# Attention output of a macaron layer: the weighed values are scaled in one VectorE product into a buffer, and GpSimd adds the buffer to x

## What is computed

```python
s = einsum('bihd,bjhd->bhij', qr, conj(kr)).real           # rotated queries and keys
maha = maximum(qn[..., None] + E*E * kn[:, :, None, :] - 2.0 * E * s, 0.0) / V
logits = coef * log1p(maha / nu) - 0.5 * DH * log(V)        # E = exp(-mu |i-j|), V from E
A = softmax(where(causal, logits, -inf), axis=-1)
out = einsum('bhij,bjhd->bihd', A, v)
x = x + concat(out.real, out.imag) @ Wo                     # summed over the heads
```

## Time and profile before

| | us |
|---|---|
| median of 3 runs | 1686.04 (1684.88 to 1686.15) |
| profiled execution, own time | 1685.38 |
| its span | 1683.6 |
| TensorE busy | 1624.1 (96%) |
| VectorE busy | 1494.5 (89%) |
| ScalarE busy | 1443.1 (86%) |
| GpSimd busy | 1013.6 (60%) |

### The profile page before, as it was taken

How to read it: one execution, slowest core, us unless ns; L and a number is a source line. 1 busy time by engine, 2 the same in 40 slices (tenths; PEclk the granted TensorE clock), 3 DMA queues, 4 the chain that set the end, 5 groups by cost and what they waited for, 6 DMA issues and landing times. The chain is left out here.

```text
span 1683.6 us, 31247 instructions
## 1 busy us (share of the span) xinstructions
PE 1624.1 (96%) x9690; PEld 1227.8 (73%) x9690; DVE 1494.5 (89%) x3380; ACT 1443.1 (86%) x2909; POOL 1013.6 (60%) x954
## 2 busy tenths in 40 slices
PE   5999988999999999999999999999999999899998
PEld 4787865777776777677777777777776776677876
DVE  6878878999999999999999999999999989977665
ACT  6677678999999999999999999999999998765765
POOL 3564556666666666665766666666666656245555
PEclk9999999999999999999999999999999999999999
DMA  6000022232223323232222323232232322100000
GB/s 178 1 1 1 1 97 73 64 92 64 76 70 76 79 64 85 58 82 70 75 74 64 92 64 76 55 92 69 74 84 60 80 59 51 26 8 7 13 13 13
DMA packets 50484, 100.05 MB, mean 59 GB/s; under 512 B 8208, under 2 KB 25872, under 8 KB 50320
## 3 DMA queue, kind: packets, MB, share of 16 engines
q1 hardware_dynamic: 50320, 98.07, 22.7%
HBM read 17.95 MB, written 5.24 MB: 14 GB/s over the span
## 5 line engine op out<-in xcount | busy, mean ns | idle before, releaser
L1500 POOL TENSOR_TENSOR early<-early 128x1024 f32<-128x1024 f32 x127 | 303.7, 2391 | 421.4 <-PE pS L1191 227.6
L661 POOL TENSOR_TENSOR hid_lo_d<-hid_d,hid_hi_d 128x512 fp32r<-128x512 f32 x176 | 231.4, 1315 | 218.4 <-ACT hid_hi_d L566 211.8
L1392 ACT ACTIVATE early<-early,qnorm 128x128 f32<-128x128 f32 (+3 forms) x512 | 246.6, 552 | 68.0 <-DVE early L1591 67.3
L1191 PE MATMUL pS<-early 128*128 128x128 f32 (+3 forms) x1024 | 297.6, 433 | 0.4 <-PEq L115 0.4
L1376 ACT ACTIVATE early<-early,nmax 128x128 f32<-128x128 f32 (+3 forms) x512 | 280.9, 558 | 7.7 <-DVE nmax L1578 7.4
L1191 PEld LDWEIGHTS pS<-early 128*128 128x128 f32 x1024 | 164.7, 191 | 96.1 <-issue 61.4
L1587 DVE SCALAR_TENSOR_TENSOR pS<-pS,ek 128x1280 f32<-128x1280 f32 x128 | 190.9, 1492 | 43.5 <-PE pS L1191 41.9
L1509 POOL TENSOR_TENSOR ek<-early 128x128 f32<-128x128 f32 (+3 forms) x256 | 216.1, 877 | 3.0 <-ACT early L1384 2.6
L1509 POOL TENSOR_TENSOR ek<-decay,early 128x128 f32<-128x128 f32 (+3 forms) x256 | 215.0, 873 | 0.0
L1233 PE MATMUL pS<-ident,early 128*128 128x128 f32 x1280 | 184.9, 278 | 13.3 <-DVE early L1591 7.0
L1405 ACT ACTIVATE early<-early,params 128x512 f32<-128x512 f32 (+1 forms) x256 | 196.4, 816 | 0.0
(11 more groups left out here) (393 smaller groups left out, 3752.5 us busy)
## 6 DMA issues: line engine op xcount, KB each, us to landing
early<-early SPq DMA_DIRECT2D x263, 256.0 KB, 3.4
early<-trig_d SPq DMA_DIRECT2D x64, 64.0 KB, 2.0
trig_d<-early SPq DMA_DIRECT2D x3, 1024.0 KB, 6.9
early<-in_w SPq DMA_DIRECT2D x3, 704.0 KB, 8.7
x_sb<-in_x SPq DMA_DIRECT2D x4, 512.0 KB, 8.3
early<-in_wqk SPq DMA_DIRECT2D x16, 128.0 KB, 3.4
cos<-trig_d SPq DMA_DIRECT2D x32, 64.0 KB, 2.2
sin<-trig_d SPq DMA_DIRECT2D x32, 64.0 KB, 2.0
```

Of the source, the lines that this page charges most:

```text
L661: g.tensor_tensor(hid_lo[:, par], hid[:, par], hid_hi[:, par].bitcast(F32), ALU.subtract).then_inc(lo_done, 1)
L1191: last = pe.matmul(s.pS[:, span(I)], rot[:, I * P:(I + 1) * P], rot[:, N:N + (I + 1) * P], start=True, stop=True)
L1392: last = a.activation(u[:, span(I)], u[:, span(I)], ACT.Relu, bias=qnorm[:, r % 2, I:I + 1])
L1500: g.tensor_tensor(rot[:], by_cos[:], crossed[:], ALU.add).then_inc(S["rot_done"], 1)
```

## The change

VectorE no longer adds to x. One TENSOR_TENSOR of 512 columns (`normalise_out`) multiplies `p7` by the reciprocals, each spread over 128 columns, into a new SBUF buffer `weighed`, and signals `y_done`. It stands where the first two tiles' additions stood, ahead of `distances`. GpSimd's step now begins with `accumulate`: it waits for `y_done` and adds `weighed` to x, 512 columns in one TENSOR_TENSOR, and signals `acc_done`. TensorE's `weigh` waits for `y_done` in place of `acc_done`, and `normalise_out` waits for the `acc_done` of the pair before, since there is one `weighed`. To make room, `q_turned` moves into columns of `dist` that the attention doesn't read.

```diff
-        q_turned = sb("q_turned", [P, 2, P])
+        q_turned = s.dist[:, 2 * N:SW].rearrange("p (k d) -> p k d", k=2)
+        weighed = sb("weighed", [P, TILES, P])
...
-                wait(pe, S["acc_done"], n)
+                wait(pe, S["y_done"], n)
...
+            def accumulate(i, r):
+                n, b = i * 16 + r, r % B
+                g.wait_ge(S["y_done"], n + 1)
+                xb = s.x_sb[:, b * TILES:(b + 1) * TILES, :]
+                g.tensor_tensor(xb, xb, weighed[:], ALU.add).then_inc(S["acc_done"], 1)
+
             def a_step(i, r):
+                if live(i, r - 3):
+                    accumulate(i, r - 3)
...
-            def accumulate(i, r, tiles=range(TILES)):
-                n, b = i * 16 + r, r % B
+            def normalise_out(i, r):
+                n = i * 16 + r
                 v.wait_ge(S["av_done"], n + 1)
                 v.wait_ge(S["rinv_done"], n + 1)
-                for I in tiles:
-                    xt = s.x_sb[:, b * TILES + I, :]
-                    last = v.scalar_tensor_tensor(xt, s.p7[:, I * P:(I + 1) * P], rinv[:, r % 4, I:I + 1], xt,
-                                                  ALU.mult, ALU.add)
-                if TILES - 1 in tiles:
-                    last.then_inc(S["acc_done"], 1)
+                wait(v, S["acc_done"], n)
+                v.tensor_tensor(weighed[:], s.p7.rearrange("p (c d) -> p c d", c=TILES),
+                                rinv[:, r % 4, :].unsqueeze(2).broadcast_to([P, TILES, P]), ALU.mult).then_inc(S["y_done"], 1)
...
                 if n == PAIRS:
-                    accumulate(i, r - 3)
+                    normalise_out(i, r - 3)
...
                     if live(i, r - 3):
-                        accumulate(i, r - 3, range(TILES // 2))
+                        normalise_out(i, r - 3)
                     distances(i, r)
...
-                if live(i, r - 3) and n != PAIRS:
-                    accumulate(i, r - 3, range(TILES // 2 if live(i, r) else 0, TILES))
+                if live(i, r - 3) and n > PAIRS:
+                    normalise_out(i, r - 3)
```

More of the change, by code:

```diff
@@ L1831, in program @@
                  "ek_done s_done w_done t_done relu_done ln_done zred_done exp_done v_done "
-                 "qt_done val_done tr_done trc_done av_done rinv_done acc_done stat_done dve_passed pool_passed sp_passed "
+                 "y_done qt_done val_done tr_done trc_done av_done rinv_done acc_done stat_done dve_passed pool_passed sp_passed "
                  "late_stat late_mv late_var late_ln late_root late_rstd late_step late_xn late_xt late_hi late_lo mv_done expanded0 expanded1")
```

## The result

The kernel after the change takes 1722.08 us (median of 4 runs, 1720.12 to 1723.06) against 1686.1 (4 runs): a ratio of 1.0213 with an interval of [1.0196, 1.0231], so it is slower: 36 us, where 25 were forecast.

What follows compares the result with a forecast made beforehand. Short steps bound by a ring through ScalarE and `peaks`, long ones by TensorE. 25.8 (short steps) - 1.4 + 0 + 1.6 = 26.0 us on 1685.4, with the median 0.7 above, hence 1711; range 1696 to 1728.

Steps and rivals of the forecast that it cites:

- The ring: Short steps: `distances`, ScalarE's clamp to logarithm, `peaks`, additions, `distances` again; 8.69 us, growing to 8.77 with the product.
- the gain behind the transpose: Two VectorE additions removed there, 0.48 us; in short steps covered by the wait for ScalarE, so no gain.
- The rival that VectorE is the bound: Short steps: less VectorE work makes them faster, down to TensorE's 8.51 us; 1668 in all; chance 0.06.
- the rival that GpSimd's idle time covers the addition: Short steps: `peaks` sees no more of `ek`, steps take 8.77 us, 1684 in all; chance 0.08.
- The collision: Short steps: late `rotate` makes `ek` run into `peaks`, 0.51 us each, read between 0.47 and 0.85 in two steps.
- The sign that the prediction named: Short steps in the profile after: a 384-column piece of `peaks` at 1.07 us would show the forecast right.
- The first short steps: First short step of each of 7 blocks: product done early, 0.2 us off each, -1.4 in all.
- Long steps and last head: Long steps: 0, at most 2 us in all; steps 120 to 127: VectorE's 0.48 gain set against the collision, 0.
- a sign that the reserve is not enough: Long steps over 9.9 us would mean VectorE's idle time there does not cover the change; 9.86 was expected.
- The end: Pairs 126 and 127: `moments` waits for GpSimd, some 1.1 us each, 0.8 counted on the path: +1.6.
- a `rotate` 0.3 later: Short steps: `rotate` 0.3 us later than forecast, steps 9.54 us, 1726 in all; chance 0.07.
- The rival of whole instructions: Short steps: `peaks` waits for whole GpSimd instructions, steps take 9.8 us, 1739 in all; chance 0.06.

Runs made afterwards that it cites:

- E1: The changed kernel with GpSimd's addition cut to 8 of 128 columns of each tile, product and waits kept: 1681.39 us, ratio 0.9983 to the kernel before.
- E7: The changed kernel with more dummy products on TensorE in the two long waits at the end: 1719.66 us, ratio 1.0201 to the kernel before.
- E3: The changed kernel with GpSimd's addition behind `qnorm` instead of ahead of `rotate`, except in the last head: 1727.36 us, ratio 1.0258 to the kernel before.
- Z0: Z1 without the wait of GpSimd's addition for the end of `peaks`: 1712.65 us, ratio 1.0166 to the kernel before.
- E4: The changed kernel with `peaks` of the 56 short steps reading `p7` in PSUM, not its SBUF table: 1707.82 us, ratio 1.0136 to the kernel before.
- Z1: The changed kernel with product behind the transpose, GpSimd's addition a step later after `peaks`, last head's additions on VectorE: 1678.85 us, ratio 0.9968 to the kernel before.

## Why the prediction was right, and what it got wrong

**The ring.** Right: `peaks` at 6.27 behind `distances`, the gain behind the transpose turned into idle time (0.66), the product at 0.60, 8.78 without a collision in E1. The rival that VectorE is the bound fell with that; the rival that GpSimd's idle time covers the addition fell because `y_done` comes late and `rotate` starts at 1.41 (1.47 forecast; GpSimd woke 0.08 after the product's end, not 0.14).

**The collision, mis-sized.** I took 0.51 from a line between n = 58 and n = 60. There is no such line. In each of the 56 short steps exactly one piece of `peaks` waits, for exactly one instruction of GpSimd, the last of `ek`: the cost is about 0.63 if it is the 128-column piece and 0.47 if it is the 384-column one, 0.57 in the mean (35 and 21 of 56). So a step takes 8.77 + 0.57 = 9.34 and not 9.28, and the 56 steps cost 28.9 us and not 25.8: the 3.1, with the 1.4 below, are the 4.5 in the table. That 0.51 came so near to 0.57 is luck, since the line behind it joins a step with one wait and a step with two. n = 60 in the earlier trace rows cost 0.85 because two pieces waited there, each for another instruction of `ek`, 0.73 for 0.35 and 1.07 for 0.61 (kernel before):

```profile
831.41 0.73 DVE L1578 CUSTOM_DVE_ANT_0 early<-early,lam,params 128x128 f32<-128x128 f32 x1
...
832.07 1.07 DVE L1578 CUSTOM_DVE_ANT_0 early<-early,lam,params 128x384 f32<-128x384 f32 x1
```

After the change, which piece waits turns on hundredths: `ek`'s third piece lets go at just about the time at which `peaks` starts, and either `ek`'s last piece or the first piece of `peaks` gets in first. What tips it is not settled; the 384-column piece waited in 21 steps here, in 27 in the second profile of the same kernel and in 12 in E7's. The sign that the prediction named, a 384-column piece at 1.07, thus shows in a part of the steps only.

**The first short steps.** The 1.4 us that I took off did not come: `rotate` starts at 1.41 there too. The last long step now overruns, VectorE has no idle time in it, and the product is done no earlier.

**Long steps and last head.** I set 0 with 2 as the upper bound; 1.9 came, nearly all of it in the last long step of six of the seven blocks, and by another mechanism: two builds of tables on VectorE meet `ek` there. These six steps take 10.11 to 10.32, over the 9.9 that the prediction named as a sign that the reserve is not enough. VectorE at the end of such a step (n = 55):

```profile
798.54 0.85 DVE L1559 TENSOR_TENSOR wqk_lo<-early,wqk_hi 128x256 fp32r<-128x256 f32 x1
799.31 0.95 DVE L1572 TENSOR_SCALAR early<-early,params 128x512 f32<-128x512 f32 x1
```

In the kernel before these take 0.39 and 0.54; the 0.87 together is more than the reserve there holds. The last head lost 0.8, where I had set VectorE's gain against the collision: the 1.87 of the normalising products is of the same kind, and I had not seen it.

**The end.** The waits of `moments` are 1.38 and 1.39, a little under the forecast's 0.14 + 1.28 + 0.1 = 1.52. No row stood behind the 0.1 for the way back; here `moments` starts 0.03 behind the addition's end. What I missed is that they lengthen TensorE's idle times and that its clock falls behind them: of the 5.3 us of the changed kernel's profile beside E7 (231.36 less 226.07) 2.9 went with E7's dummy products and 2.4 stayed, against 1.6. All terms together: 4.5 + 1.9 + 0.8 + 3.5 + 0.2 makes the 11 us between forecast and result. That the result still lies in the range is luck in part: its upper end was set for a `rotate` 0.3 later, and `rotate` was on time.

**The rival of whole instructions.** I gave it 0.06 and argued that a loss of 0.47 does not show blocking for all of a GpSimd instruction. That reading was wrong, and the earlier trace rows held the answer. Take a piece's own duration off its end: that is when it began to read. Set it beside the recorded end of the GpSimd instruction that was running:

| where | piece began | GpSimd's instruction ended | apart |
|---|---|---|---|
| before, n = 58 | 813.83 + 1.07 - 0.61 = 814.29 | 811.04 + 3.46 = 814.50 | 0.21 |
| after, n = 58 | 828.01 + 0.98 - 0.35 = 828.64 | 828.11 + 0.74 = 828.85 | 0.21 |
| after, n = 59 | 837.70 + 1.08 - 0.61 = 838.17 | 837.51 + 0.85 = 838.36 | 0.19 |
| E3, n = 58 | 829.23 + 1.22 - 0.35 = 830.10 | 829.01 + 1.29 = 830.30 | 0.20 |
| Z0 | 830.62 + 1.75 - 0.74 = 831.63 | 830.28 + 1.54 = 831.82 | 0.19 |

Whatever the length of the wait, 0.46 to 1.01 us, the piece begins 0.2 ahead of the recorded end; in all 56 short steps of the changed kernel it is 0.19 to 0.21. So a piece waits for the whole of the instruction in GpSimd's hand. GpSimd waits in its turn: in the 21 steps in which the first piece of `peaks` gets in first, `ek`'s last piece takes 0.83 to 0.86, as in n = 59, and in the other 35 it takes 0.72 to 0.76, as in n = 58. The Trainium skill, "SBUF — State Buffer", section "Who interferes with whom", says just this ("fully blocks"), and E4 bears out its condition of two SBUF inputs for `peaks`. What the rival's 1739 had wrong was the count: it had two pieces wait in every step, and `ek`'s third piece lets go just in time for the first.

## What to carry to other kernels

When work goes to GpSimd, ask what GpSimd will have in hand when a VectorE instruction with two SBUF inputs starts: each meeting costs the rest of that one instruction, so price it by instruction and count the meetings, and don't draw a line through two of them. The place counts more than the amount: the same product and addition took 36 us in one place and gave back 5 in another, where the product filled a known wait, the addition was kept out of `peaks`' way and the last head kept its additions on VectorE. And an addition that somebody waits for at once, such as the mean of the finished x, belongs on the engine that waits: in Z1, which leaves those on VectorE, what lies behind the last `distances` takes 226.13, as in the kernel before (226.07), and not 231.12.

## What the hardware showed that I had not expected

- A TENSOR_SCALAR with one SBUF tensor as input, besides its scalars, is held up by GpSimd too: 0.95 for 0.54 us at 512 float32 columns, and 3.98 for 2.11 for eight of 128, both with `ek` running beside them. So one SBUF input does not by itself keep an instruction clear; `peaks` with its second input in PSUM (E4) was clear.
- The granted clock fell to 1.2 GHz behind TensorE waits of 2.53 and 3.01 us at the end of the attention, for 3.42 and 6.83 us, where waits of 1.09 and 1.53 had left it up; with the waits filled it stayed at 1.00.
